# One whole-array product for four quarter products in the scan of a linear-attention kernel

## The reference, cut to what matters

```python
v_old = jnp.einsum('bhd,bhde->bhe', k_t, state)
delta = jnp.clip(v_t - v_old, -CLAMP, CLAMP)
update = jnp.clip(BETA * k_t[..., :, None] * delta[..., None, :], -CLAMP, CLAMP)
state = state + update
...
o = jnp.clip(jnp.einsum('bhij,bhj->bhi', state, q_t), -CLAMP, CLAMP)
```

## Time and profile before

| | us |
|---|---|
| median of 3 runs | 1407.27 |
| lowest, highest | 1399.64, 1412.8 |
| span of the profiled execution | 1464.6 |
| of it the scan | 24 to 1203 |
| TensorE matmul busy | 1274.9 (87%) |
| VectorE busy | 1034.3 (71%) |
| GpSimd busy | 909.4 (62%) |
| ScalarE busy | 817.4 (56%) |

### The profile page before, as it was taken

One profiled execution on the slowest core, in us unless ns is written; L12 is line 12 of the kernel. 1 busy time (PEld: TensorE's weight loads), 2 busy tenths in 40 slices (PEclk: granted clock), 3 DMA queues, 4 the chain that ended last, 5 costly groups with the idle time before them and its releaser, 6 DMA issues.

```text
span 1464.6 us, 47170 instructions
## 1 busy us (share of the span) xinstructions
PE 1274.9 (87%) x18561; PEld 836.0 (57%) x18561; DVE 1034.3 (71%) x4437; ACT 817.4 (56%) x2193; POOL 909.4 (62%) x1320
## 2 busy tenths in 40 slices
PE   7877778898989898998989899999998889898886
PEld 3333545555646665666656575656566565666654
DVE  4768787788758768787767878787777855564442
ACT  3232353556566566667565656475663737566754
POOL 5345767677857576676766676667746546665431
PEclk8677778999979899899979998899989979999998
DMA  6000000101010000000010000000001010101000
GB/s 167 2 1 13 27 18 17 32 8 29 8 29 8 21 14 17 17 17 23 8 29 6 15 21 14 20 9 23 12 11 28 9 29 10 30 17 30 4 3 7
DMA packets 27256, 29.34 MB, mean 20 GB/s; under 512 B 12145, under 2 KB 22290, under 8 KB 27026
## 3 DMA queue, kind: packets, MB, share of 16 engines
q0 software_dynamic: 8336, 16.73, 4.6%
q1 hardware_dynamic: 18690, 9.51, 2.4%
HBM read 24.90 MB, written 2.29 MB: 19 GB/s over the span
## 4 chain that ended last, share of the span: by engine, by line
PE 41%; POOL 13%; issue 11%; DVE 11%; ACT 6%; another core or an unknown queue 1%; DMA 0%; POOLq 0%; DVEq 0%; ACTq 0%
PE ps L703 3%; PE ps L759 3%; POOL sb L1866 3%; PE ps L536 2%; PE ps L924 2%; PE ps L826 2%; PE ps L605 2%; PE ps L616 1%; PE ps L805 1%; PE ps L746 1%; PE ps L915 1%; DVE ps L1036 1%; PE ps L783 1%; PE ps L829 1%; PE ps L591 1%
## 5 line engine op out<-in xcount | busy, mean ns | idle before, releaser
L1866 POOL DMA_INDIRECT sb<-table,sb x240 | 241.5, 1006 | 82.5 <-issue 50.0
L1036 DVE TENSOR_TENSOR_SCAN ps<-ps,sb 128x47 f32<-128x47 f32 (+3 forms) x1024 | 270.8, 264 | 30.3 <-ACT sb L1439 1.5
L1028 DVE TENSOR_TENSOR ps<-sb,ps 128x24 f32<-128x24 f32 (+3 forms) x1024 | 193.3, 189 | 14.7
L536 PE MATMUL ps<-sb 128*128 128x512 bf16 x585 | 184.6, 427 | 10.9 <-ACT sb L1651 2.8
L1726 POOL TENSOR_TENSOR sb<-sb 128x1 f32<-128x1 f32 x128 | 72.9, 572 | 160.6 <-DVE sb L971 158.8
L605 PE MATMUL ps<-sb 32*32 32x32 f32 x2032 | 70.3, 209 | 42.8 <-DVE sb L1008 33.8
L605 PEld LDWEIGHTS ps<-sb 32*32 32x32 f32 x2032 | 41.4, 109 | 113.3 <-DVE sb L1008 66.8
L616 PEld LDWEIGHTS ps<-sb 32*32 32x32 f32 x2032 | 41.5, 108 | 99.5 <-DVE sb L1044 60.6
L1363 ACT ACTIVATE sb<-ps 128x128 f32<-128x128 f32 x128 | 35.1, 276 | 103.6 <-PE ps L559 96.4
L536 PEld LDWEIGHTS ps<-sb 128*128 128x128 bf16 x585 | 56.0, 107 | 64.7 <-issue 20.4
L977 DVE TENSOR_TENSOR sb<-ps,sb 128x128 f32<-128x128 f32 x112 | 32.2, 288 | 83.5 <-PE ps L887 29.5
(11 more groups left out here) (308 smaller groups left out, 3609.4 us busy)
## 6 DMA issues: line engine op xcount, KB each, us to landing
sb<-table,sb POOLq DMA_INDIRECT x240
sb<-in_cs SPq DMA_DIRECT2D x16, 128.0 KB
table<-sb SPq DMA_DIRECT2D x17, 64.0 KB, 1.5
sb<-dscr SPq DMA_DIRECT2D x64, 2.0 KB
out<-sb SPq DMA_DIRECT2D x16, 64.0 KB
sb<-in_x SPq DMA_DIRECT2D x3, 256.0 KB, 5.8
sb<-in_wex SPq DMA_DIRECT2D x1, 512.0 KB, 3.9
sb<-in_rvx SPq DMA_DIRECT2D x1, 512.0 KB, 4.2
```

The lines of the kernel that those rows point to most:

```text
L536: e.matmul(b[:, 0:512], onesb[:, :], onesb[:, :].unsqueeze(1).to_broadcast([128, 4, 128]), start=True, stop=True)
L1028: e.tensor_tensor(at(psP, p + ROW - 3 - 2 * m, [ROW, 3], [2, m], [1, 2]), AC[:, row(n, k), :, HIST - 2 * m:HIST].rearrange("p r (a b) -> p ...
L1036: e.tensor_tensor_scan(at(psD, 16 + k + COMB * skip, [COMB, 3 * ROW - skip]), at(psP, p + skip, [1, 3 * ROW - skip]), Q[:, i % 32, skip:3 ...
L1866: e.indirect_dma_start(GA[:, k, :], None, table[0:128 * i + 128, :] if i else table0, bass.IndirectOffsetOnAxis(u[:, k:k + 1], 0)).then_in ...
```

## The change

The second product becomes one fp32 product over all 128 rows and columns of the array. For that its stationary operand `SB` becomes 128x128: the 32 columns of the state are read four times over and multiplied with `blk`, the 128x128 mask that is 1 where row and column belong to the same head. The product's moving operand (12 columns), its result (128x12) and every place in the order stay. Before the product TensorE also waits, once in the program, for the constants to be loaded. `FILL` is printed in shorter lines, its 2250 digits are the same, and `ORDER` is untouched.

```diff
-    SB, R, DS = two([128, 32]), two([128, 32]), two([128, 128])
+    SB, R, DS = two([128, 128]), two([128, 32]), two([128, 128])
...
-                    for q in range(4):
-                        rows = slice(32 * q, 32 * q + 32)
-                        x = e.matmul(b[rows, 0:12], SB[g % 2][rows, :],
-                                     KM[c2 % 2][rows, 4 * o2:4 * o2 + 4, :].rearrange("p a b -> p (a b)"), start=True,
-                                     stop=True)
-                    x.then_inc(sc.mm, 1)
+                    w.wait_ge(*loaded("cst"))
+                    e.matmul(b[:, 0:12], SB[g % 2][:, :], KM[c2 % 2][:, 4 * o2:4 * o2 + 4, :].rearrange("p a b -> p (a b)"),
+                             start=True, stop=True).then_inc(sc.mm, 1)
...
-                        e.tensor_tensor(SB[g % 2][:, :], psS[:, 0:32], blk4, ALU.mult).then_inc(sc.mask, 1)
+                        e.tensor_tensor(SB[g % 2][:, :].rearrange("p (q d) -> p q d", q=4),
+                                        psS[:, 0:32].unsqueeze(1).to_broadcast([128, 4, 32]),
+                                        blk.rearrange("p (q d) -> p q d", q=4), ALU.mult).then_inc(sc.mask, 1)
```

More of the change, by code:

```diff
@@ L200 @@
 FILL = (
[L201 to L220, removed]
@@ L221 @@
-    "0920000920")
+    "091909062040000000025030020020010000010010000100100000010000500001020020000070000901000001020000000000000020"
+    "200002000200000000000000000010010001000000100500002000000000000000200000000000000000000000000000400000000001"
+    "000000000010000000000110030000000000010000000000100000000020000000000000000000000000000520000000030000000300"
+    "000000000000002000020000000010000000000000000000101000000000000000000000000000010000000000000200000000030000"
+    "000000000000000002020000000000000200000000000300020000000000010000000000000000000001300000000000000000000000"
@@ new lines @@
+    "000000000000000000000000001003001010000000000100300000006000100000000000000000000000000000000000000000000000"
+    "000000000000000020000000000000000000000000000100000000000002000000000000003220000000030103000000100300200000"
+    "000000000000000000000000000000000000000000000002200000000000000000000000000000000000000000000010000000000010"
+    "000000000000003000000000000000000000000000000000000000004030000000000000000000001000000000000000000000000000"
+    "000000004000000000000000000000500000000000000000012000000000003000000000100000000000000000100000000000000000"
@@ new lines @@
+    "400000000000000000000000000000000000000000200000000000000000000000000020000520000000006030000000000002000000"
+    "000000000000000000000000000000000000000000000000000000000000000000000400000000200000000000000330090006000000"
+    "000000000000000000000000000000005000000000000000000000000000000000000000000000000000000000000000000003000000"
+    "040000000000000020020003000213000080000000000000000000000000000000000000000000000000000000000000000010000000"
+    "000000000002000000001000000000001040000000000001000000000000301000300000005000000000000000000000000100000000"
@@ new lines @@
+    "000000000000000000000000000000000000000000000000000000000000000100000000000000000041000000060000000000000050"
+    "000000000100000010000000000000200000000000000200040000000000000000000000000000000000000000000000005000000000"
+    "820930000000000000020100000000000000000000000000004000100000000000000000200000000000000000000400000000020000"
+    "009300472001000000000000000000000000000000000000000000200000000000000000000000000000000000000000062540000100"
+    "010000901000010200000000000000100000000000000000000000000000100000000000020000000300000000000000000000000000"
@@ L226, in program @@
+    "000000001200023000700160100000000001020000000000920005000000920930000200004200000920000920")
 def program(nc, t):
```

## The result

The changed kernel takes 1420.28 us against 1406.11 us, medians of 8 runs each: ratio 1.010, interval 1.0072 to 1.0127, so 14 us slower. The forecast was 1419.

The account below looks back on a forecast made before the run. VectorE and TensorE hand the scan to and fro, neither with much slack, later mostly TensorE's queue. 5.5 + 3.5 + 2.3 + 1.3 + 0 = +12.6 us, 0.86%, so 1407.27 becomes 1419 us; forecast's own range 1410 to 1430, overall 1394 to 1440.

Parts of the forecast that it names:

- The mask's price: VectorE's mask at 128x128 takes 288 ns against 181, +0.107 us a block; 5.5 + 3.5 us counted on the path.
- the early term: Before 248 us, 67 wider masks at 0.107 us make 7.2 us; VectorE is 77% busy, so 5.5 us count.
- the late one: Behind 248 us, only the 33 masks on the chain of waits count for the wider mask: 3.5 us.
- The product's latency: Second product ends 0.14 us later; costs 2.3 us in 16 early blocks and 1.3 us in nine later ones.
- TensorE's own time: Gains and losses around the chain's 110 second products behind 248 us, by neighbouring records: taken as 0.
- The prices at entry and exit: Second product on TensorE: entry behind whole-array records saves 0.09 us; exit saves 0.04 or costs 0.07, 0.15 before narrow operands.
- whole to narrow lies about at 0: Second products between a whole-array record and a narrow-operand one, 16 on the chain, neither gain nor lose on TensorE.
- faster rival: TensorE's queue alone sets the pace and quarters were the price: 14.8 us saved, 1393 us; chance 0.14.
- -1.7 to +3.7: Range in us for TensorE's gains and losses around the chain's second products behind 248 us; 0 was taken.
- total of 12.6: Sum over the scan, 5.5 + 3.5 + 2.3 + 1.3 + 0 = +12.6 us, 0.86% of the profiled span.
- All of VectorE's time landing: Slower rival: the masks' 27.2 us and 8.5 us of longer waits land in full, +36 us, 1441 us; chance 0.20.
- no change: Rival: VectorE's idle quarter swallows the mask, TensorE's gains pay for its losses, 1407 to 1410 us; chance 0.18.

Follow-up runs that it names:

- the control: The kernel before, unchanged, run and profiled again on a chip where it takes 1403.2 us: ratio 0.998, profiled span 1402.9 us.
- the third set's chip: Kernel before 1404.0 us; against it the whole change 1.0105, only the first 67 blocks changed 1.0109, only the other 187 changed 1.0066.
- the first set's: Kernel before 1468.7 us; against it wide mask only 1.0029, whole-array product only 0.9952, change in first 67 blocks 1.0033, in other 187 blocks 1.0011.

## Why the prediction was right, point by point

*The mask's price.* 0.107 us was right as a duration (0.099 measured), wrong as a cost: 0.04 of it falls into the 0.30 us that the next multiplication waits for the scan instruction. The step "67 x 0.107, of which 77% count" should have used start to start, 0.066; by that the early term is 3.4 us and not 5.5, the late one 2.2 and not 3.5. Measured alone, the mask costs 4.2 us (0.3% in both sets; both intervals end below 0.6%); the forecast's terms for it were 9.0.

*The product's latency*, 2.3 + 1.3 us, and *TensorE's own time*, 0: together 3.6 us, measured alone 4.1 (1.0029) on a chip with the result's time. The prices at entry and exit came out within a hundredth where the clock is full. The sum has three gaps, though. It counts TensorE's own time only for the products on the chain behind 248 us and gives the first 67 blocks none, while in 42 of these the next record follows directly and comes, all together, 3.8 to 4.4 us later than in the control (4.0 with the product alone, nothing with the mask alone); the 0.09 at the entry can give back at most a part. It has no price at the lower clock, at which 25 of those 67 products run. And "whole to narrow lies about at 0" does not follow from its own prices, -0.09 and +0.15, nor does the faster rival's saving of 0.04 there; the measured exit, 0.27 us in the median behind 248 us against 0.18, makes it 0 all the same. That the sum is right on one chip and of the wrong sign on the other (0.9952) suggests that the zero was a balance, not known to better than the -1.7 to +3.7 given.

*What the sum left out.* Mask and product are two steps of one way, so the add can come late by both, 0.099 + 0.14 us, and at the lower clock by 0.099 + 0.30. The forecast charged the product's 0.14 only where VectorE stood waiting already. In the changed kernel's chain, which goes back to 249 us, there are 51 masks, and in the control's, back to 245 us, 34; 44 adds, and 35. The masks' time on it is 10.5 us against 3.9. The first and last mask in the changed kernel's:

```profile
249.74 0.19 DVE sb L1041
...
1157.15 0.16 DVE sb L1041
```

The 3 to 6 us by which the whole exceeds its halves is about what the mask was overcharged. So the total of 12.6 came out right in part by luck: the mask was charged too much, and the interplay of the two halves and TensorE's early time were charged at nothing. The direction, both mechanisms and TensorE's prices at full clock were right by themselves. That the interplay is the add coming late by both is argued, not shown by a run.

*The place.* The forecast laid 7.8 us before 248 us and 4.8 behind. Applied alone, the first 67 blocks cost 15 and the rest 9 on the third set's chip. It looks as if a loss made early took the place of one that would be made later, which the method, adding blocks up, can't see. That a late block in the first 370 us costs more than its own length goes with the granted clock there, 0.84 in the control, 0.83 with the mask alone, 0.81 with the product alone and 0.78 to 0.82 in every profile with both halves: the product, not the mask, goes with the lower clock. Whether the clock is the cause or follows from TensorE's longer waits was not tried.

*The rivals.* All of VectorE's time landing (+36 us) is out, and so is no change. The faster rival's claim, that the drained array was the price, fails on the chips with the result's time; on the first set's, with the mask left narrow, the kernel is 0.5% faster, about half of what the rival counted.

*What was to be seen.* The mask at 279 ns, the product at 0.29 to 0.39 us, the record behind four others at 0.44: as told. VectorE was to be busy 27 us more and is 18 more (the mask's group 25 more): the wide mask's last 0.08 us run beside the next multiplication (122.42 to 122.50). VectorE's waits for the second product were to grow by 8 us and fell by 8, as they would if VectorE came later itself. Blocks before 248 us were to be 0.1 us slower each; by the 65th the changed kernel is 2 to 7 us behind in its three profiles, so 0.03 to 0.1.

## What to carry to other kernels

Price an instruction on an in-order engine by the distance from its neighbour's start to the next start, not by its duration: one that stands where its successor waits for something else is partly free, and there is the place for extra work. A change that lengthens two steps of one round trip can cost more than the two measured alone. Price a TensorE product at the clock that it will run at: the same one was 0.39 us long at full clock and 0.60 at half. Before two profiles are compared, compare their spans with the runs: a span 4% above them belongs to other conditions, and only a profile of the old kernel taken beside the new one can be held against it.

## What was not expected of the hardware

The same program takes 1403 us on two of the chips used and 1468 on another, with mean granted clocks of 0.931 and 0.904 over its runs, and VectorE's durations alike (the wide mask 279 ns on the one, 280 on the other); a change's worth can differ there by more than its interval (0.9952 against 1.0029). A 128x64 fp32 copy in SBUF took 190 ns in the median and up to 2.6 us beside GpSimd. Between a scan instruction and the multiplication that needs it, VectorE has a slot for another instruction: the narrow mask starts 0.17 us after the first (121.79 to 121.96) and the multiplication 0.13 after the mask, with the same 0.30 in all as without it. A whole-array fp32 product of 12 columns loses twice as much against the quarters at half the clock (0.30 us against 0.14).
